# Block-diagonal keys stored batch by batch instead of head by head, in a gated cross-attention and expert layer

## The reference, cut to what matters

```
xn  = layer_norm(layer_norm(x)) * g + b          xfn = layer_norm(ctx) * g + b
q   = (xn @ Wq + bq)   in 16 heads of 8          k, v = (xfn @ Wk + bk), (xfn @ Wv + bv)
w   = softmax(q k^T / sqrt(8))                   128 x 77 for each batch and head
x   = x + tanh(g_xattn) * (w @ v)
h   = relu(layer_norm(x) @ w1[e]) ** 2           for each of 8 experts e
x   = x + tanh(g_ffn) * sum over the top 2 experts of prob_e * (h @ w2[e])
```

## Time and profile before

| | us |
|---|---|
| median of three runs | 310.99 |
| profiled execution | 310.82 |
| its span | 309.0 |
| TensorE busy | 286.2 (93%) |
| VectorE busy | 231.6 (75%) |
| ScalarE busy | 179.2 (58%) |
| GpSimd busy | 112.4 (36%) |

### The profile page before, as it was taken

The page is one execution under the profiler, slowest core; times in us unless marked ns, Lnnn a source line. Parts: engine busy times, 40 slices in busy tenths (PEclk is TensorE's granted clock), DMA queues, the critical chain, the costliest instruction groups (busy, mean ns, idle before and its releaser), DMA issues.

```text
span 309.0 us, 7855 instructions
## 1 busy us (share of the span) xinstructions
PE 286.2 (93%) x2837; PEld 235.2 (76%) x2837; DVE 231.6 (75%) x934; ACT 179.2 (58%) x412; POOL 112.4 (36%) x211
## 2 busy tenths in 40 slices
PE   7887889799999999999999999999999999989894
PEld 5555467577878888888888888888788787878784
DVE  7887687788688977888698868886668666646765
ACT  0533656555665676565656665567656555655573
POOL 6594543473156323652166116422612211221110
PEclk9999999999999999999999999999999999999998
DMA  3362301193529363934575275727391620070011
GB/s 71 96 160 59 64 6 51 35 134 110 224 45 118 74 180 139 130 79 127 188 118 101 72 243 76 94 60 249 64 108 35 204 87 3 6 304 6 0 36 34
DMA packets 19078, 30.83 MB, mean 100 GB/s; under 512 B 5321, under 2 KB 11626, under 8 KB 19040
## 3 DMA queue, kind: packets, MB, share of 16 engines
q1 hardware_dynamic: 12144, 22.35, 30.5%
q0 software_dynamic: 3408, 6.61, 9.3%
q10 hardware_dynamic: 3488, 1.38, 1.7%
HBM read 18.94 MB, written 2.21 MB: 68 GB/s over the span
## 4 chain that ended last, share of the span: by engine, by line
PE 56%; DVE 25%; issue 8%; ACT 4%; ACTq 2%; POOL 2%; DMA 1%; SPq 1%; DVEq 0%; POOLq 0%
PE y L596 14%; PE c L551 9%; PE ab L507 6%; DVE u L1160 4%; PE s L528 3%; DVE negm L1043 3%; PE ab L574 3%; PE ab L566 2%; PE h L589 2%; PE h L591 2%; PE h L590 2%; PE ab L457 2%; DVE o L1066 2%; DVE m_parts L1050 2%; DVE st L1078 2%
## 5 line engine op out<-in xcount | busy, mean ns | idle before, releaser
L822 ACT ACTIVATE p<-s 77x512 f32<-77x512 f32 x128 | 74.4, 583 | 18.7 <-PE s L528 18.5
L1043 DVE TENSOR_REDUCE negm<-ab 128x4 f32<-128x308 f32 x128 | 60.4, 474 | 32.6 <-PE ab L507 30.6
L528 PEld LDWEIGHTS s<-qs,ks 104*77 104x77 f32 x512 | 54.0, 148 | 11.6 <-issue 3.7
L596 PE MATMUL y<-w2s,hs 128*128 128x128 f32 x448 | 60.4, 279 | 2.6 <-ACT hs L827 2.6
L528 PE MATMUL s<-qs,ks 104*77 104x128 f32 x512 | 59.2, 238 | 0.6 <-ACT p L822 0.6
L596 PEld LDWEIGHTS y<-w2s,hs 128*128 128x128 f32 x448 | 55.4, 193 | 4.6 <-ACT hs L827 3.7
L1388 POOL TENSOR_SCALAR rs<-mv 128x1 f32<-128x1 f32 x32 | 7.3, 228 | 131.6 <-DVE mv L1082 131.6
L507 PE MATMUL ab<-ks,qs 96*128 96x312 f32 x128 | 49.4, 387 | 4.8 <-DVE negm L1043 1.6
L827 ACT ACTIVATE hs<-u 128x512 f32<-128x512 f32 x56 | 34.9, 624 | 13.6 <-DVE u L1160 13.6
L1160 DVE SCALAR_TENSOR_TENSOR u<-h,gb 128x512 f32<-128x512 f32 x56 | 37.8, 677 | 1.9 <-PE h L591 1.5
L551 PE MATMUL c<-p,vs 77*32 77x128 f32 x1024 | 34.6, 276 | 0.0
(11 more groups left out here) (128 smaller groups left out, 500.6 us busy)
## 6 DMA issues: line engine op xcount, KB each, us to landing
gb<-gates_scratch SPq DMA_DIRECT2D x14, 768.0 KB, 5.7
gb<-gates_scratch SPq DMA_DIRECT2D x14, 256.0 KB, 3.5
qs<-q_hi SPq DMA_DIRECT2D x12, 256.0 KB, 7.6
out_dram<-y_out POOLq DMA_DIRECT2D x7, 256.0 KB, 6.4
x_sb<-in_x_dram POOLq DMA_DIRECT2D x6, 256.0 KB, 3.5
qs<-q_lo SPq DMA_DIRECT2D x6, 256.0 KB, 9.3
ks<-k_hi SPq DMA_DIRECT2D x34, 39.0 KB
ks<-k_lo POOLq DMA_DIRECT2D x32, 39.0 KB, 3.2
```

The costliest lines, as they stand in the source:

```text
L528: mm = nc.tensor.matmul(p[0:N, T * i:T * i + T], ks[:, par, c, i, NP * j:NP * j + N], qs[:, par, c, T * j:T * j + T], start=True, stop=True)
L596: mm = nc.tensor.matmul(bank_y[:, D * b:D * b + D], hs[:, e % 2, T * b:T * b + T], w2s[:, e, :], start=(e == 0 and b == 0), stop=(e == E - ...
L822: nc.scalar.activation(p32[:, m % LR, :], src, ACT.Exp).then_inc(p_done, 1)
L1043: nc.vector.tensor_reduce(negm[:, :, c], bank_ab[bank][:, 0:J * NP].rearrange("t (i n) -> t i n", n=NP)[:, :, 0:N], AX.X, ALU.max, negate= ...
```

## The change

The axes of `ks` behind `c` are swapped: instead of head, then batch, it is now batch, then head. The four heads of a batch lie side by side, 312 columns in one piece. The two readers take the same columns from their new places. The writers now cut each transfer by batch: the destination of one DMA is 8 rows with 16 pieces (4 `c` times 4 batches) of 78 elements, so a DMA of 39 KB goes as 128 pieces of 312 bytes. The number of DMAs, their bytes, their order and all waits are as before. The ones are written in 312-byte pieces too, 32 per DMA instead of 8 of 1248.

```diff
-        ks = sb("ks", [MR, 2, NC, J, G * NP], F32R)
+        ks = sb("ks", [MR, 2, NC, G, J, NP], F32R)
...
-                        sp.dma_start(ks[r:r + HD, par, :, i, :].bitcast(F32),
-                                     k_hi[QROWS * i:QROWS * i + QROWS].rearrange("p b n -> p (b n)").bitcast(F32))\
+                        sp.dma_start(ks[r:r + HD, par, :, :, i, :].rearrange("p c b n -> p (c b) n").bitcast(F32),
+                                     k_hi[QROWS * i:QROWS * i + QROWS].bitcast(F32))\
                             .then_inc(k_stacked[par], 16)
...
-                    sp.dma_start(ks[r:r + SPLITS, par, :, i, :].bitcast(F32),
-                                 ones[:, :].rearrange("p (o n) -> p o n", o=1).broadcast_to([SPLITS, NC, G * NP]))\
+                    sp.dma_start(ks[r:r + SPLITS, par, :, :, i, :].rearrange("p c b n -> p (c b) n").bitcast(F32),
+                                 ones[:, 0:NP].rearrange("p (o n) -> p o n", o=1)
+                                 .broadcast_to([SPLITS, NC * G, NP]))\
...
-                nc.tensor.matmul(p[:, 0:J * NP].rearrange("t (i n) -> t i n", n=NP), qs[0:QR, par, c, T * j:T * j + T],
-                                 ks[0:QR, par, c, :, NP * j:NP * j + NP], start=True, stop=True).then_inc(ready, 1)
+                nc.tensor.matmul(p[:, 0:J * NP], qs[0:QR, par, c, T * j:T * j + T],
+                                 ks[0:QR, par, c, j].rearrange("p i n -> p (i n)"), start=True,
+                                 stop=True).then_inc(ready, 1)
...
-                    mm = nc.tensor.matmul(p[0:N, T * i:T * i + T], ks[:, par, c, i, NP * j:NP * j + N],
+                    mm = nc.tensor.matmul(p[0:N, T * i:T * i + T], ks[:, par, c, j, i, 0:N],
                                           qs[:, par, c, T * j:T * j + T], start=True, stop=True)
...
-                    pool.dma_start(ks[r:r + HD, par, :, i, :].bitcast(F32),
-                                   k_lo[QROWS * i:QROWS * i + QROWS].rearrange("p b n -> p (b n)").bitcast(F32))\
+                    pool.dma_start(ks[r:r + HD, par, :, :, i, :].rearrange("p c b n -> p (c b) n").bitcast(F32),
+                                   k_lo[QROWS * i:QROWS * i + QROWS].bitcast(F32))\
                         .then_inc(k_lo_stacked[par], 16)
```

## The result

The changed kernel takes 333.06 us (median of 4 runs, 331.77 to 335.86) against 311.6 (4 runs) for the kernel before: a ratio of 1.071, 95% interval 1.065 to 1.077, some 21.5 us slower. The profiled execution took 332.65 us, 21.8 more than that of before. The forecast of 311.5 with a range up to 315.5 was wrong; what happened is its rival A, only much larger than priced there. A few executions of some kernels are slower at a lower clock; the ratios leave them out, the medians keep them.

The account below looks back on a forecast made before the run. TensorE was taken to bound the kernel (busy 286.2 of 309.0 us, 56% of the chain; DMA 1%). Terms -0.2 + 0.2 + 0.5 = +0.5 on 310.82 gave 311.3, with the median 0.17 above: 311.5, range 309.8 to 315.5.

Parts of the forecast that it names:

- rival A: Tiles 2 to 7: pieces make landings late, TensorE stalls where slack is little; 315.7 us with L = 2.0; chance 0.30.
- The score matmul: Line 507's 128 matmuls: one piece instead of four saves 3 ns each, -0.2 us on the chain, ends 0 and -1.9.
- The issues: Key DMA issues: SyncE's don't grow with pieces; GpSimd's grow by 50 to 110 ns each, bounds 0 and +320.
- rival C: GpSimd's key issues grow by 320 ns, so tile 0's keys land 1.9 us late; 313 or a little more; chance 0.06.
- The transfers: Key DMAs of 128 pieces instead of 32: last landing 0.9 us later in tiles 2 to 7, stalling only tile 7, 0.2 us.
- L: Lateness of the last landing in tiles 2 to 7, taken as 0.9 us.
- lower bound: Added transfer time zero: 128 small packets at 20.6 ns would be 2.6 engine-microseconds, less than the present 3.2 per DMA.
- upper bound: All added pieces come on top, spread over eight engines: 0.25 us per DMA, 3.0 us for a tile of 12 DMAs.
- far bound: All 96 added pieces of a key DMA cost 20.6 ns each on top: 2.0 engine-microseconds per DMA.
- The software queue: GpSimd's key DMAs: the queue already joins four pieces in a packet and may well join sixteen.
- The sum over the slacks: Tiles 2 to 7: lateness 0.9 us against slacks of 0.9, 0.9, 1.7, 2.5, 1.9, 0.7; only tile 7 stalls, 0.2 us.
- Tile 0: First score matmul, nothing hides its key transfers: six longer GpSimd issues and one DMA's added time, +0.5 us, ends 0 and 3.4.

Follow-up runs that it names:

- the better order: GpSimd's low keys written in head order 2, 3, 0, 1: on the changed kernel 317.09 us, ratio 1.018; on the kernel before 311.16 us, ratio 0.998.
- late-alone kernel: Kernel before, large pieces, with only the key DMAs of tiles 3 to 7 (and queries behind them) issued 2.9 us later: 319.62 us, ratio 1.026.
- 1, 2, 3, 0: Changed kernel with GpSimd's low keys in the head order 1, 2, 3, 0 instead of 0, 1, 2, 3: 324.61 us, ratio 1.039.

## Why the prediction was wrong, point by point

**The score matmul.** Right: forecast 3 ns each and nothing else; measured 3, and 312.16 against 311.22 with the transfers left as they were. By the Trainium skill's rule the pieces would have cost 12 ns; these runs show 3.

**The issues.** SyncE's: forecast zero, measured 686 ns against 672, right. GpSimd's: forecast +50 to +110 ns; the rows that answer to the earlier trace rows are

```profile
L1418 POOL DMA_DIRECT2D ks<-k_lo x32: 632/696/842, 12.2 to 241.9; - x32
...
L1423 POOL DMA_DIRECT2D ks<-k_hi x30: 779/846/952, 14.8 to 244.3; - x30
```

+152 and +302 in the median, so the last issue ends 0.8 us later; it starts 0.4 us later (1.3 in tile 5). The line through `x_sb` and `ctx_sb` was too flat; both shapes have other dimensions, and which of these counts was not tested. My bound of +320 held for the medians. The sign named for rival C, an issue over 0.7 us, did show in the third band, but C's price was 313 and the later ends of the issues can carry at most 0.9 of the 3.6 us of lateness.

**The transfers.** This is the step that failed. "I take L = 0.9 us for the lateness of the last landing in tiles 2 to 7, nearer to the lower bound, since the row of small packets lies there." It was 3.6 on average, above even the upper bound of 3.0 in four of the six tiles. The late keys then made TensorE wait in all six tiles and not in tile 7 alone. The keys-only stretch of tile 1 in the changed kernel, 37.5 to 45.0 us, answers to the earlier trace rows:

```profile
DMA packets 928, 0.48 MB, mean 65 GB/s; under 512 B 800, under 2 KB 864, under 8 KB 928
...
q0 software_dynamic: 384, 0.32, 31.7%
q1 hardware_dynamic: 544, 0.16, 22.2%
```

31.7% + 22.2% of 16 engines for 7.5 us is 64.7 engine-microseconds, 5.4 per DMA of 39 KB against 3.2. The 96 added pieces cost 2.2, or 22 ns each: a little more than "all 96 added pieces come on top", which I had as the far bound (20.6 ns each, 2.0). The lower bound came from an average that no packet had. Of the 805 packets of first loads in the earlier trace rows, 292 are of 4 bytes and took 8 ns each, and 513 are of 512 bytes and took 28; the 323 bytes and 20.6 ns are their mean. 128 pieces at 28 ns are 3.5 engine-microseconds, more than the 3.2 of before, so there was no bound at zero. And the hardware queue's 544 packets in the stretch above took 49 ns each on average (22.2% of 16 engines for 7.5 us), not 20.6. Two more things were left out. The queries were put down as "not changed", and `q_lo` landed 3.3 us later after its issue. And I compared bytes and packets and never asked where they go; but the order of the heads moves both kernels alike, and the new layout would land 3.1 us later in the better order too.

**The software queue.** I wrote that it may join sixteen pieces. It joins 14: q0 has 992 packets more, 16 for each of the 62 DMAs, and there are still 64 over 2 KB in tile 1 (928 less 864), now of 4368 bytes each, with 64 of 624 bytes beside them that hold the other two. The hardware queue got exactly the 3456 packets forecast.

**The sum over the slacks.** The working was right. It is nearly flat until L = 0.9 and then steep, so a range for the time needed both ends of L, and mine stopped at L = 2. The table of rival A gave 9.4 us for L = 3.0. With the measured L of each tile it gives 2.9 + 2.3 + 3.5 + 0.4 + 1.8 + 2.1 = 13.0, and 13.8 were measured. The late-alone kernel confirms it from the other side.

**Tile 0.** Forecast +0.5, with an end of 3.4; measured +2.8. Nothing hides it; six DMAs go out on each queue, and the last lands 10.4 us after the first issue where it took 7.6.

**The clock.** Not in the prediction at all. About 5 of the 21.5 us are its part; with the one stall of 0.2 us that I forecast there was nothing to look for.

What stays open: why a small piece costs 22 ns of a DMA engine; why 1, 2, 3, 0 lies between the two other orders, and with it whether rows 32 apart are what collides; and why four DMAs on the hardware queue cost as much as eight on the software queue. Tile 0 does not profit from the order (10.3 us from first issue to last landing against 10.4), and that wasn't followed up.

## What to carry to other kernels

A transfer that takes 1% of the chain can be within a microsecond of leading it: before making transfers costlier, measure landing against first reader for every tile, and price the change at both ends of the bound. The matmul did not care about four pieces of 312 bytes, the DMA engines cared a great deal, so stay with long pieces in the transfer and let TensorE do the stepping. When two queues fill bands of one buffer at the same time, try another order of destinations in one of them. A shift by two heads cost nothing here and made the landings 1.5 to 2.0 us earlier in tiles 2 to 7; a shift by one brought 1.0 with small pieces, and tile 0 gained nothing. And an average over packets is no price: look at their sizes first.

## What the runs showed of the hardware that was not expected

- Splitting a 39 KB on-chip copy from 32 to 128 pieces raised its engine time from 3.2 to 5.4 engine-microseconds (tile 1, keys alone). The Trainium skill ("DMA: Bandwidth & Descriptors", "Why small descriptors are slow (HBM only)") says that copies within on-chip memory don't suffer from small pieces; these do.
- Key transfers of two queues hold each other up by where they write: shifting GpSimd's destinations by two heads took SyncE's queue in tile 1 from 22.2% to 16.4% of 16 engines and the kernel from 333 to 317 us, shifting its sources did nothing. With 1248-byte pieces the landings moved as well, from 13.8 to 12.3 us.
- A GpSimd DMA issue with 128 pieces took 696 ns (low part) and 846 ns (third band) in the median against 544 with 32, while SyncE's went from 672 to 686.
- A TensorE wait of 3.2 us was followed by 6.8 us at 1.2 GHz, in which 54 matmuls ran; in the next 6.8 us, at 2.4 GHz, it was 81. If both stretches held like work, a third of 6.8, some 2.3 us, was lost once more; this is an estimate from these two rows.
